# Folding the second row stage of a graph network into its first edge walk, and one-hot matrices made once for all heads

## The reference

```python
def gat_layer(x, W, a_l, a_r, b, src, dst, num_nodes):
    z = (x @ W).reshape(num_nodes, heads, d)
    el = jnp.einsum('nhd,hd->nh', z, a_l)
    er = jnp.einsum('nhd,hd->nh', z, a_r)
    e = el[src] + er[dst]
    e = jnp.where(e > 0, e, 0.2 * e)
    m = jax.ops.segment_max(e, dst, num_segments=num_nodes)
    ex = jnp.exp(e - m[dst])
    alpha = ex / jax.ops.segment_sum(ex, dst, num_segments=num_nodes)[dst]
    return jax.ops.segment_sum(z[src] * alpha[:, :, None], dst, num_segments=num_nodes) + b
h = relu(gat_layer(layernorm(x), W1, al1, ar1, b1, src, dst, N).reshape(N, 256))
out = gat_layer(h, W2, al2, ar2, b2, src, dst, N)[:, 0, :]
```

## Time and profile before

| | us |
|---|---|
| median of 3 runs | 5027.19 (5023.35 to 5033.29) |
| the profiled execution | 5031.31 |
| its span, first to last instruction | 5029.7 |
| plan and rows1 | 0 to 166 |
| walk1 | 166 to 1206 |
| rows2 | 1206 to 1362 |
| walk2 | 1362 to about 2397 |
| walk3 | 3373 to 4372 |

### The profile page before, as it was taken

The page is one execution under the profiler, slowest core; times in us unless marked ns, Lnnn a source line. Parts: engine busy times, 40 slices in busy tenths (PEclk is TensorE's granted clock), DMA queues, the critical chain, the costliest instruction groups (busy, mean ns, idle before and its releaser), DMA issues. The chain is left out here.

```text
span 5029.7 us, 64428 instructions
## 1 busy us (share of the span) xinstructions
PE 3132.8 (62%) x14424; PEld 2042.4 (41%) x14424; DVE 1986.2 (39%) x7900; ACT 782.0 (16%) x2089; POOL 2786.7 (55%) x2845
## 2 busy tenths in 40 slices
PE   4476676776466666666321999306666666565799
PEld 3355555554333333333310777203333333233566
DVE  4466666664144444444640111342121221166222
ACT  2100101001200000100100333111001010144223
POOL 1577777772177777776335000467777777542121
PEclk9688878777777777777555999657777777787899
DMA  5555555554444444444534666654444444443221
GB/s 153 142 146 146 145 145 147 144 144 91 87 127 128 127 128 128 129 129 106 149 114 124 212 213 214 175 165 114 113 114 113 113 114 113 105 128 106 63 63 49
DMA packets 391822, 649.53 MB, mean 129 GB/s; under 512 B 104252, under 2 KB 253070, under 8 KB 390946
## 3 DMA queue, kind: packets, MB, share of 16 engines
q0 software_dynamic: 144128, 410.22, 31.7%
q1 hardware_dynamic: 211858, 200.79, 13.5%
q10 hardware_dynamic: 35728, 37.50, 2.4%
HBM read 513.91 MB, written 134.34 MB: 129 GB/s over the span
## 5 line engine op out<-in xcount | busy, mean ns | idle before, releaser
L509 PE MATMUL walk_ps_part<-walk_rows,walk_whot 128*80 128x129 f32 (+1 forms) x6272 | 1705.1, 426 | 862.7 <-DMA walk_rows<-h,walk_idx 569.3
L509 PEld LDWEIGHTS walk_ps_part<-walk_rows,walk_whot 128*80 128x80 f32 x6272 | 1037.3, 194 | 1366.8 <-issue 591.1
L399 POOL DMA_INDIRECT walk_rows<-z_one_head,walk_idx x784 | 764.5, 975 | 281.5 <-issue 227.9
L399 POOL DMA_INDIRECT walk_rows<-z_two_heads,walk_idx x784 | 764.0, 975 | 238.7 <-issue 235.4
L399 POOL DMA_INDIRECT walk_rows<-h,walk_idx x784 | 743.0, 948 | 256.0 <-issue 237.6
L636 DVE TENSOR_SCALAR walk_whot<-keep_winx,walk_dloc,walk_w 128x80 f32<-128x80 f32 x2352 | 570.1, 332 | 0.0
L434 ACT ACTIVATE walk_window<-walk_ps_part 80x257 f32<-80x257 f32 (+1 forms) x294 | 112.3, 382 | 1811.7 <-PE walk_ps_part L509 1805.8
L632 DVE COPY walk_carry<-keep_carry 80x1 f32 (+1 forms) x245 | 32.8, 158 | 757.9 <-ACT walk_weight L422 757.9
L471 PE MATMUL walk_ps_el_rows<-keep_ident,walk_rows 128*32 128x128 f32 (+1 forms) x98 | 32.1, 327 | 417.3 <-DMA walk_rows<-z_one_head,walk_idx 277.5
L1284 POOL DMA_DIRECT2D y_slots<-exp_y x54 | 38.7, 716 | 416.6 <-DVE exp_y L1350 377.0
L1323 PE MATMUL exp_ps_hid<-exp_hT,exp_w 128*128 128x256 f32 x864 | 221.8, 390 | 23.1 <-DMA exp_b<-in_ffn_b 22.5
(11 more groups left out here) (303 smaller groups left out, 3649.6 us busy)
## 6 DMA issues: line engine op xcount, KB each, us to landing
exp_w<-in_ffn_W SPq DMA_DIRECT2D x108, 512.0 KB
walk_dstB<-dst SPq DMA_DIRECT2D x196, 160.0 KB
agg<-walk_window ACTq DMA_DIRECT2D x198, 80.3 KB
h_slots<-walk_clear SPq DMA_DIRECT2D x98, 148.0 KB
exp_h<-h_slots SPq DMA_DIRECT2D x54, 256.0 KB
y_slots<-exp_y POOLq DMA_DIRECT2D x54, 256.0 KB, 5.9
walk_rows<-z_two_heads,walk_idx POOLq DMA_INDIRECT x784
walk_rows<-z_one_head,walk_idx POOLq DMA_INDIRECT x784
```

Of the source, the lines that this page charges most:

```text
L399: pool.indirect_dma_start(out=Z[k // 2][:, k % 2 * GROUP_TILES + t, :], out_offset=None, in_=table, in_offset=bass.IndirectOffsetOnAxis(ap ...
L509: last = pe.matmul(P[k % 2][0:WIN, cols], S[k % HOTS][:, h, t, :], Z[k // 2][:, k % 2 * GROUP_TILES + t, h * HS:h * HS + HW], start=t == 0 ...
```

## The change

rows2 is gone. Its work is done in walk1, a unit of 128 nodes a pair, by `SecondRows`: unit v has the nodes from (v - 3) x 128, so that its sums are complete when pair v comes; the first three units work on spare rows. Three units are left for a loop behind the walk. If a table check in plan finds that the nodes come too late in the order of the edges, all units are done in that loop.

In walk1 SP loads a unit's sums (`load`), after two waits: the windows up to pair v - 2 must be stored, and a buffer free. It stores the unit before (`store`) and waits until that has landed. ACT waits before the first `window` of pair p until the sums of unit p + 1 have been loaded. The edge inputs have four buffers and are loaded for three pairs ahead of the loop. `rr` is one DMA a step. ACT waits for the weights of the second layer before it copies the first indices.

For the weighting, DVE makes one plain one-hot matrix for the 8 tiles of a step (`hot`, 128 x 640) and multiplies it per head by the weights (128 x 640), both TENSOR_TENSOR with one operand in PSUM. In walk3 ACT weights it, eight operations a step. In `logits` and `maxima` some copies and drains go.

```diff
 def edge_walk(...)          # sync, walk1 and walk2
-                def load(p, q, used):
-                    if used is not None:
-                        sp.wait_ge(cols1, used)
+                def load(p, q):
+                    sp.wait_ge(cols4, p + 1)
...
-                        for h in range(H):
-                            for c in range(2):
-                                sp.dma_start(rr[q][0:1, c, h, part],
-                                             dram["rr"][c:c + 1, bass.ds(g * GROUP_TILES, GROUP_TILES)]) \
-                                  .then_inc(inputs[q], 16)
+                        sp.dma_start(rr[q][:, :, :, j, :],
+                                     dram["rr"][one, :].rearrange("o (c h t) -> o c h t", c=2, h=2)[:, :, 0:H, :]) \
+                          .then_inc(inputs[q], 16)
...
-                load(0, 0, None)
+                for p in range(AHEAD + 1):
+                    load(p, p)
+                if node:
+                    node.start_sp(sp)
+                    node.load(sp, 0, 0, unit_row(sp, 0), None, None)
                 with sp.Fori(0, n) as i:
                     for m in range(1, PAIRS + 1):
-                        load(i * PAIRS + m, m % 2, i * PAIRS + m)
+                        p = i * PAIRS + m
+                        load(p + AHEAD, (m + AHEAD) % INS)
+                        if node:
+                            node.load(sp, p, m % 2, unit_row(sp, p), stored, i * (32 * PAIRS) + (32 * m - 16))
+                            node.store(sp, p - 1, (m - 1) % 2, i * (PAIRS // 2) + (m - 1) // 2, unit_row(sp, p - 1))
...
             with act.Fori(0, n) as i:
                 for m in range(PAIRS):
+                    if node:
+                        node.head(act, p, m % 2)
+                        act.wait_ge(node.agg_in[(m + 1) % 2], i * (8 * PAIRS) + 16 * ((m + 1) // 2 + 1))
                     window(i * UNROLL + 2 * m, ...)
+                    if node:
+                        node.copy_out(act, p, m % 2)
                     if gat:
                         exps(i * PAIRS + (m + 1), (m + 1) % 2)
...
             def pair(p, m, s, turn, ahead):            # tensor
                 products(s, 2 * m, 1)
+                if node:
+                    node.turn(pe, p, m % 2)
                 products(s, 2 * m, 2)
                 turn_el(p + 1, b, turn)
                 products(s, 2 * m, 3)
+                if node:
+                    node.products(pe, p, m % 2)
                 turn_ends(p + 1)
...
             def pair(p, m, s, loaded, half):           # vector
-                spread(p, q, s, loaded)
-                maxima(p, q)
+                spread(m % INS, s, loaded)
+                hot(s, 2 * m % UNROLL)
+                hot(s + 1, (2 * m + 1) % UNROLL)
+                maxima(p, m % INS)
+                if node and m:
+                    node.split(dve, p - 1, 1 - q)
                 logits(p, m % PAIRS)
                 dve.wait_ge(w_ready, p + 1)
                 hots(s, 2 * m % UNROLL, W[q])
                 hots(s + 1, (2 * m + 1) % UNROLL, W[q])
+                if node:
+                    node.scale(dve, p, q, half)
...
-                for h in range(H):
-                    for t in range(GROUP_TILES):
-                        last = dve.tensor_scalar(S[k % HOTS][:, h, t, :], keep["winx"][:, :], dloc[k][:, t:t + 1],
-                                                 w[:, h, col:col + 1] if gat else weight[k][:, t:t + 1],
-                                                 ALU.is_equal, ALU.mult)
+                for h in range(H if gat else 0):
+                    last = dve.tensor_tensor(S[k % HOTS][:, h, :, :], S0[k % HOTS][:, :, :],
+                                             Wp[:, h, part].unsqueeze(2).to_broadcast([128, GROUP_TILES, WIN]), ALU.mult)
```

More of the change, by code:

```diff
@@ L276, in edge_walk @@
+def edge_walk(nc, keep, dram, name, table, heads, nodes=None):
     H, gat = max(heads, 1), heads > 0
@@ L326, in edge_walk @@
[L326 to L332 removed]
+            Cf = work[0:ROWS, WIN:WIN + TILE]
@@ L543, in _ @@
                 pair(n * PAIRS, 0, n * UNROLL, None, False)
+                if node:
+                    left, first = tail(pe)
+                    u = n * PAIRS + 1
+                    node.turn(pe, u, 1)
+                    node.products(pe, u, 1)
+                    with pe.Fori(0, left) as i:
+                        for k in range(2):
+                            node.turn(pe, i * 2 + (u + 1 + k), k)
+                            node.products(pe, i * 2 + (u + 1 + k), k)
             else:
@@ new lines, in _ @@
+                if node:
+                    node.split(dve, n * PAIRS, 0)
+                    left, first = tail(dve)
+                    u, half = n * PAIRS + 1, n * (PAIRS // 2)
+                    node.scale(dve, u, 1, half)
+                    with dve.Fori(0, left) as i:
+                        node.scale(dve, i * 2 + (u + 1), 0, i + (half + 1))
+                        node.split(dve, i * 2 + u, 1)
+                        node.scale(dve, i * 2 + (u + 2), 1, i + (half + 1))
+                        node.split(dve, i * 2 + (u + 1), 0)
+                    node.split(dve, left * 2 + u, 1)
@@ L733, in attention_rows @@
     ident = keep["ident"]
-    table, erd = dram[f"z{heads}"], dram[f"er{heads}"]
-    with Phase(nc, f"rows{layer}") as ph:
+    table, erd = dram["z2"], dram["er2"]
+    with Phase(nc, "rows1") as ph:
         Waug = ph.sb("w", [128, HALVES, AW])
@@ L835, in tail @@
                        .then_inc(z_copied4, 1)
-            if first:
-                pipeline(act, (std, 1), (tail, 0), (head, 1))
-            else:
-                pipeline(act, (tail, 0), (head, 1))
+            pipeline(act, (std, 1), (tail, 0), (head, 1))
         @block.tensor
@@ L1911, in _ @@
             chunks(dve, finish)
-PHASES = ("plan", "rows1", "walk1", "rows2", "walk2", "post", "dispatch", "experts", "combine", "walk3", "update", "route", "ffn")
+PHASES = ("plan", "rows1", "walk1", "walk2", "post", "dispatch", "experts", "combine", "walk3", "update", "route", "ffn")
 def program(nc, io, out):
```

460 lines of the change are left out of this document (315 added, 145 removed).

## The result

The changed kernel takes 5356.3 us (5346 to 5360, 4 runs), the kernel before 5030.0 in the same comparison: ratio 1.065, interval 1.063 to 1.067. It is slower by 326 us, where the prediction had 4970 and its range ended at 5065. The profiled execution took 5346.3 us.

A forecast was written before the change was run, and what follows sets the result against it. POOL's gathers bound the walks at 20.5 us a pair, but SP's ring of 21.4 us would set walk1's pace. -156 (rows2) +34 (start) +26 (tail) -1 +42 (ring) -2 = -57 us, 4970 by the median, range 4905 to 5065.

The forecast's parts named there:

- the ring: walk1: SP's stores, inputs and unit load, ACT's window and DVE's split wait in a circle; 21.4 us a pair, +42 us.
- ACT's longest wait ahead of the even window: Sign in walk1's profile after: ACT waits longest ahead of the even windows, for the unit's sums; no size given.
- hardly idle: Sign in the profile after: SP hardly idle, its waits being those on `n_er` stores of 3 to 5 us.
- the long ring: Rival in walk1: from 22.5 us a turn the gain is used up, at 24.0 the time is 5099 us; chance 0.24.
- POOL's waits over 100 us: Sign in walk1: POOL's waits forecast at about 40 us; exceeding 100 us would mean the long ring.
- The landing of the parts: Term of the ring: the unit's store of 128 rows lands after 3.7 us, 2 us of it not depending on rows.
- a ring of 18.6: walk1: with 2.0 us for both landings the ring would be an estimated 18.6 us and hidden; hidden's chance 0.25.
- The landing of the unit's load: Term of the ring: 129 KB behind 616 KB of inputs and clears land after 3.1 us, between 2.2 and 5.1.
- The inputs: Term of the ring: SP issues the inputs of two steps in 6.24 us; value load and two waits take 1.1.
- The start: Ahead of walk1: ACT waits for the second layer's weights before its first index copy, at 202.5 us; +34 us.
- The tail: Behind walk1: the last three units begin only once the last window is stored; +26 us.
- The weighting: DVE in the walks: 7.9 to 7.2 us a pair, only -1 in walk1 and -2 in walk2; gathers taken as unchanged.

The follow-up runs named there:

- e14: Changed kernel with the parts stored as rows of 512 B instead of 6 B; 5184.9 us, ratio 1.030 to the kernel before.
- e11: Changed kernel with SP issuing the unit's load ahead of the inputs; 5061.6 us, ratio 1.009 to the kernel before.
- e13: Changed kernel with the landing of the unit's stores waited for one unit later; 5220.2 us, ratio 1.037 to the kernel before.
- e12: Changed kernel with unit's load ahead of inputs, landing waited one unit later, ACT's wait for weights behind its index copies; 4939.4 us, ratio 0.984.
- e15: e12 with the clears of h_slots moved from walk1 to walk2; 4868.9 us, ratio 0.967 to the kernel before.
- e16: e15 with the weighting of the kernel before in the two attention walks; 4916.5 us, ratio 0.977 to the kernel before.
- e10: The kernel before, unchanged, run again for its trace; 5019.9 us.
- e9: The changed kernel, unchanged, run again beside the kernel before; 5339.4 us, ratio 1.064.
- e1: Changed kernel with the unit's load ahead of the inputs, where the kernel before took 5979 us; ratio 1.005.
- e8: Same kernel as e12, where the kernel before took 6039 us; ratio 0.994.
- e17: Changed kernel with only the clears of h_slots moved to walk2; 6241.2 us beside 6032.3 for the kernel before, ratio 1.035.
- e18: e15 with the parts as rows of 512 B, where the kernel before took 6032 us; 6091.0 us, ratio 1.009.
- e2: Changed kernel with the landing waited for one unit later, where the kernel before took 5979 us; ratio 1.053.
- e4: e1 with ACT's wait for the weights behind its index copies, where the kernel before took 5979 us; ratio 0.9995.
- e5: The kernel of e1 again, where the kernel before took 6039 us; ratio 0.994.

## Why the prediction was wrong

Right were the mechanism and most of its places: rows2's time gone, no gather between walk1's turns but at the ring's pace, ACT's longest wait ahead of the even window for the unit's sums, SP's wait on the parts, the rest of the program as it was. One sign was wrong by the prediction's own terms: SP is not "hardly idle" but waits 9.3 us a turn for the parts to be made, as in a ring it must while the load lands and ACT works. The rival that came true, the long ring, was named with its point (22.5 us a turn), its first cause (a store landing over 4.9 us) and its sign (POOL's waits over 100 us). It was given 0.24 and thought to end near 24 us. What failed were sizes:

- **The landing of the parts**, 3.7 us: measured 6.0. The step that failed is "taking 2 us as not depending on rows, 2 + 6.0 x 128 / 448". Of the 8.0 us of the earlier trace rows for 448 pieces of 6 B, 128 pieces keep 6.0: an estimate, a line through the two, leaves 5.2 us that don't depend on the number (the 448 stood behind a table of 453 KB, which may be part of it). The 2 us came from tiny inputs, which are loads, and nothing showed that a store of such pieces has as little. e14 shows that the pieces' size, or their distance, is the cause. The page "DMA: Bandwidth & Descriptors" of the Trainium skill (Specifications) says that under 512 B a transfer reads, modifies and writes; the runs agree in that it is 6.0 us at 6 B and 3.1 at 512 B, though none shows the reading. The prediction quoted that rule and left it out of the sum. This term makes 2.3 of the 8 us a turn. The 2.0 us by which the prediction estimated a ring of 18.6 is given by that page of the Trainium skill (Anatomy of one DMA) for DMAs that GpSimd issues; of SP's here only the table's store (2.2 us) and the load with nothing ahead (2.7, e11) come near it.
- **The landing of the unit's load**, 3.1 us: measured 5.6. The bounds were 2.2 and 5.1, and I went near the lower row because it ran beside gathers. For what counts, 616 KB issued ahead, the kernel before had no row. e11 shows the cause: 2.7 us with nothing ahead. 2.5 us a turn, and another 1.0 in the turn shown.
- **The inputs**, 7.3 us with the value load: measured 8.9. I took off three `rr` issues of 0.39 us; the one that stays takes 0.7 and not 0.35, which is 0.7 of the 1.6 us; the rest lies between the issues. And the 0.9 us a turn of SP's loop, above, had no term.
- **The landings aren't independent** of each other or of the order, which the ring as a sum of terms supposes. In e11 and e13 the load and the stores exchanged some 3 us.
- **The start**, +34: measured +40 to +43, by inputs at 4.7 us a step instead of 4.06 and weights that were used 7.2 us after their last issue instead of 5.1. The mechanism is confirmed by e12.
- **The tail**, +26: measured +40, the same landings three times; and the four pairs that POOL is ahead are worked off at the ring's pace ahead of it.
- **The weighting**, nothing: measured -16 us in walk2 beside the changed kernel and -48 in e15 against e16. I laid the 28 ns by which the walks' gathers differ from walk3's at the door of the 1024-column `spread`. Of them 21 went with the change (27 in walk1 from e10 to e9), and e16 brought back 14 in walk1 and 26 in walk2. The page "SBUF — State Buffer" of the Trainium skill (Who interferes with whom) says that VectorE's copies and tensor_scalars in their two-port mode and GpSimd lock each other out of a shared pair of ports. The direction agrees: 981 ns in e16's walk2 beside tensor_scalars from SBUF, 955 in e15's beside products with an operand in PSUM. The amounts don't: walk1 has twice as many tensor_scalars and lost 14 ns, and walk3 had as many as walk2 in the kernel before and its gathers took 947 ns, 945 without them. So e16 shows what the weighting costs, not by which mechanism.

Put together with the measured turn: (29.4 - 20.5) x 48 = 427 us, with -156 for rows2, +40, +40 and -16 that gives +335, where +326 were measured. Of the 8.0 us between 29.4 and the prediction's 21.4, the four sizes (2.3, 2.5, 1.6, 0.9) make 7.3.

## What to carry to other kernels

When work is moved into a loop on a queue that also waits for landings, write the ring down as a chain of issues and landings, take for a store's landing a row with pieces as small as its own, whatever the bytes, and for a load the row that had as much issued ahead of it; if the result is within a microsecond or two of the bound, expect it to be the ring, and look for what a pass of the loop costs the queue beside its issues. Then look at the order of issues first: what the next turn waits for goes ahead of what is two turns early (278 us here), a wait for a landing goes a turn later, and bulk stores that can be made elsewhere go there. A change that lost 6.5% held one that gained 3.3% with the same work in it.

## What the hardware showed that I had not expected

- 0.8 KB in 128 pieces of 6 B land later (6.0 us, 10.1 behind 616 KB) than 129.5 KB in pieces of 1036 B (2.2 and 5.4 us) or 64 KB in pieces of 512 B (3.1 us).
- Removing a wait of 6.0 us for these stores shortened the turn by 2.4 us; the next load took 2.7 us longer to land.
- A queue's loop is not free: one turn in four of SP's was 3.7 us longer, between its last wait and its first issue.
- Where e1 to e8, e17 and e18 ran, all kernels were some 20% slower, with gathers as short as ever (954 ns) when they ran. What came late was other engines' work while POOL issued gathers without a pause: in walk1 of e2 POOL waited 777.8 us for ACT's index. SP's input issues in e2, the first step's with gathers running beside them, the second's after the last gather at 660.76 us:

```profile
653.20 1.38 SPq L537 DMA_DIRECT2D walk_dstB<-dst  x1
657.39 0.70 SPq L539 DMA_DIRECT2D walk_erw<-er_two_heads  x1
660.94 0.71 SPq L540 DMA_DIRECT2D walk_reset<-seg_reset_twice  x1
664.00 0.69 SPq L543 DMA_DIRECT2D walk_rr<-tile_reset  x1
664.73 0.28 SPq L547 DMA_DIRECT2D h_slots<-walk_clear  x1
667.39 0.34 SPq L537 DMA_DIRECT2D walk_dstB<-dst  x1
667.93 0.32 SPq L539 DMA_DIRECT2D walk_erw<-er_two_heads  x1
```

  An issue takes 0.70 us instead of 0.34 and the next follows after 3 to 4 us instead of 0.5. In these traces walk2, nearly the same work in all kernels, took 1335 to 1356 us instead of 987. Why, the traces don't say. It makes the balance of the kernels another one: e18, which is e15 with rows of 512 B, is there 0.9% slower than the kernel before, e4 is at par with it, e5 and e8 0.6% faster, so a gain like e15's holds for the usual condition only.
